# Attention scores of a graph layer with and without the target's linear term

## What is computed

```
h = _layer_norm(x, ln1_g, ln1_b)
xl = (h @ Wl).reshape(-1, HEADS, C)          # left: the source's rows
xr = (h @ Wr).reshape(-1, HEADS, C)          # right: the target's rows
e = einsum('ehc,hc->eh', leaky_relu(xl[src] + xr[dst], 0.2), att)
m = segment_max(e, dst);  ex = exp(e - m[dst])
alpha = ex / (segment_sum(ex, dst)[dst] + 1e-16)
out = segment_sum(alpha[..., None] * xl[src], dst) + gat_bias
```

## Time and profile before

| | us |
|---|---|
| timed, median of 3 | 1217.9 |
| timed, lowest and highest | 1214.75, 1218.52 |
| span of the profiled execution | 1275.0 |
| VectorE busy in the profiled execution | 1030.6 |
| TensorE busy in the profiled execution | 1089.3 |

### The profile page before, as it was taken

How to read it: one execution, slowest core, us unless ns; L and a number is a source line. 1 busy time by engine, 2 the same in 40 slices (tenths; PEclk the granted TensorE clock), 3 DMA queues, 4 the chain that set the end, 5 groups by cost and what they waited for, 6 DMA issues and landing times.

```text
span 1275.0 us, 16061 instructions
## 1 busy us (share of the span) xinstructions
PE 1089.3 (85%) x5027; PEld 793.4 (62%) x5047; DVE 1030.6 (81%) x1478; ACT 681.0 (53%) x1264; POOL 436.6 (34%) x412
## 2 busy tenths in 40 slices
PE   3979879566766666499999999799999999999998
PEld 2578456444544444245555555598888888889896
DVE  8999999778777887899999999876766869583934
ACT  4601300465565654478888888767555674232420
POOL 2072073565555666177766665000002100000000
PEclk9989989888777876599999999799999999999999
DMA  5000001566565658266667666400000211000002
GB/s 187 34 10 15 25 10 34 150 168 173 165 173 160 181 166 193 59 165 194 194 191 195 191 191 153 141 1 18 9 9 25 65 38 46 1 18 25 1 1 82
DMA packets 43436, 122.85 MB, mean 96 GB/s; under 512 B 7838, under 2 KB 8626, under 8 KB 43352
## 3 DMA queue, kind: packets, MB, share of 16 engines
q0 software_dynamic: 29184, 93.81, 27.5%
q1 hardware_dynamic: 14168, 27.98, 6.6%
HBM read 116.13 MB, written 5.59 MB: 95 GB/s over the span
## 4 chain that ended last, share of the span: by engine, by line
PE 46%; ACT 7%; DVE 2%; issue 1%; ACTq 1%; another core or an unknown queue 0%; DVEq 0%
PE bank L891 11%; PE bank L851 8%; PE bank L837 8%; PE bank L784 7%; PE bank L907 7%; PE bank L795 5%; ACT counts L1077 3%; ACT hot L964 2%; ACT arena L962 2%; PE bank L822 1%; ACTq L1073 0%; DVE stat L1269 0%; PE bank L625 0%; DVE w_lo L1637 0%
## 5 line engine op out<-in xcount | busy, mean ns | idle before, releaser
L587 POOL DMA_INDIRECT arena<-left_table,arena x352 | 356.8, 1013 | 235.7 <-issue 85.4
L784 PE MATMUL bank<-arena,hot 128*128 128x512 f32 x352 | 177.5, 620 | 0.9 <-DVE den_parts L1661 0.9
L718 PE MATMUL bank<-xr_hi,hot_t 128*128 x176 | 94.9, 539 | 97.3 <-ACT bank L1050 66.7
L1569 DVE SCALAR_TENSOR_TENSOR arena<-bank,arena 128x1024 f32<-128x1024 f32 x88 | 107.7, 1224 | 54.4 <-PE bank L718 29.9
L891 PE MATMUL bank<-counts_r,ns 128*128 128x512 f32 (+2 forms) x720 | 137.1, 349 | 0.0
L891 PEld LDWEIGHTS bank<-counts_r,ns 128*128 128x128 f32 x720 | 125.6, 188 | 10.4
L1077 ACT ACTIVATE counts<-bank 128x1280 f32 x88 | 108.9, 1238 | 37.6 <-issue 21.1
L795 PE MATMUL bank<-arena 128*128 128x512 bf16 (+1 forms) x508 | 110.0, 349 | 9.2 <-ACT counts L1077 5.6
L1050 ACT ACTIVATE bank<-arena 128x1024 f32<-128x1024 f32 x88 | 90.2, 1025 | 42.8 <-DMA arena<-left_table,arena 29.9
L718 PEld LDWEIGHTS bank<-xr_hi,hot_t 128*128 128x128 f32 x176 | 41.9, 238 | 110.4 <-issue 104.9
L1573 DVE TENSOR_REDUCE arena<-arena 128x16 f32<-128x1024 f32 x88 | 107.3, 1220 | 2.7
(11 more groups left out here) (258 smaller groups left out, 2256.2 us busy)
## 6 DMA issues: line engine op xcount, KB each, us to landing
arena<-left_table,arena POOLq DMA_INDIRECT x352
arena<-in_x_dram SPq DMA_DIRECT2D x18, 256.0 KB, 5.0
arena<-in_L_gnn_W_dram SPq DMA_DIRECT2D x8, 512.0 KB
arena<-in_L_gnn_W_dram SPq DMA_DIRECT2D x2, 1536.0 KB, 11.1
arena<-in_L_gnn_W_dram SPq DMA_DIRECT2D x3, 1024.0 KB, 5.3
left_table<-arena SPq DMA_DIRECT2D x10, 260.0 KB, 2.0
out_dram<-state SPq DMA_DIRECT2D x9, 256.0 KB
arena<-in_L_gnn_Wl_dram SPq DMA_DIRECT2D x1, 1024.0 KB, 9.0
```

The lines of the kernel that those rows point to most:

```text
L587: g.indirect_dma_start(out=gathered[n % DEPTH][:, i, :], out_offset=None, in_=left_table, in_offset=bass.IndirectOffsetOnAxis(ap=src_of[:, ...
L718: ins_ = t.matmul(bank[:, rows_at(n) + i, :], mine, part[:, bass.ds(at, 1), :].rearrange("p b n -> p (b n)"), start=False, stop=(part is x ...
L784: t.matmul(bank[:, psum, :], as_float(hot[c % 4]), w[:, i, :], start=(i == 0), stop=(i == 1))
L1569: v.scalar_tensor_tensor(y, bank[:, at:at + 2, :], 0.0, over(att_relu, 1, 2), ALU.max, ALU.mult).then_inc(*rows_weighted.up())
```

## The change

The target's linear term is no longer formed, added or stored; the softmax over the edges of a target is the same without it. With it go: the linear tile and the right half of wa; the product and the reduction on VectorE for the right side; half the columns of L658; two of ScalarE's three small copies per block, with the wait between them; the subtraction L1376; the two products L731 of each pair, linear_added, keep_targets and the waits for both; and the additions L1552 and L1558. tile_ready now counts one a block instead of two. lay_scores keeps one addition and runs at the pairs of LAY_AT (12, 23, 34, 45, 56, 67, 78 and 87), two tiles after the last of its 22 tiles. The arena's tiles behind linear and wa lie lower by their size.

```diff
@@ -90,10 +90,9 @@
 
     rows_at = lambda n: 2 * ((n + ZRING - 1) % ZRING)
     QUAD = 2 * PAIR
-    LINEAR_TILES = 256 // (2 * HEADS)
 
     RUNS = 2
-    ADD_AT = {min(NG - 1, LINEAR_TILES // 2 * -(-RUNS * SK * (u + 1) // LINEAR_TILES)): u for u in range(SG // RUNS)}
+    LAY_AT = {min(NG - 1, RUNS * SK * (u + 1) // 2 + 1): u for u in range(SG // RUNS)}
     COUNT_AT = 5 * 512
     W1_PARTS = 2 * KC
     BATCH, QUARTET = 16, 4
...
@@ -651,11 +648,11 @@
                         ins_.then_inc(*projected.up())
                         if side == 0:
                             yield
-                    t.wait_ge(att_folded.sem, 2)
+                    t.wait_ge(att_folded.sem, 1)
                     if b >= 2:
-                        t.wait_ge(tile_ready.sem, 2 * (b - 1))
+                        t.wait_ge(tile_ready.sem, b - 1)
                     for k in range(KC):
-                        ins_ = t.matmul(bank[:, 4 + b % 2, 0:2 * HEADS], trans[b % 3][:, k, :], wa[:, k, :, :].rearrange("p i h -> p (i h)"), start=(k == 0), stop=(k == KC - 1))
+                        ins_ = t.matmul(bank[:, 4 + b % 2, 0:HEADS], trans[b % 3][:, k, :], wa[:, k, :], start=(k == 0), stop=(k == KC - 1))
                     ins_.then_inc(*att_projected.up())
                     yield
 
...
@@ -718,21 +715,10 @@
                         ins_ = t.matmul(bank[:, rows_at(n) + i, :], mine, part[:, bass.ds(at, 1), :].rearrange("p b n -> p (b n)"),
                                         start=False, stop=(part is xr_lo), skip_group_check=True)
                 ins_.then_inc(*rows_added.up())
-                c = 2 * n
-                if c % LINEAR_TILES == 0 and c:
-                    t.wait_ge(targets_kept.sem, c // LINEAR_TILES)
-
                 for _ in range(2):
                     t.matmul(bank[:, 7, 256:512], iota_node[:, 0:P], iota_node[:, 0:256], start=True, stop=True)
-                for i in range(2):
-                    c = 2 * n + i
-                    mine = hot_t[n // 2 % 2][:, (n % 2 * 2 + i) * P:(n % 2 * 2 + i + 1) * P]
-                    at_column = c % LINEAR_TILES * 2 * HEADS
-                    ins_ = t.matmul(bank[:, 7, at_column:at_column + 2 * HEADS], mine,
-                                    linear[:, bass.ds(at, 1), :, :].rearrange("p b w h -> p (b w h)"), start=True, stop=True, skip_group_check=True)
-                ins_.then_inc(*linear_added.up())
-
-            t.wait_ge(tile_ready.sem, 2 * NB)
+
+            t.wait_ge(tile_ready.sem, NB)
             prime(range(KEY_BANKS, 2 * ZRING))
             spread_local(0)
             t.wait_ge(keys_laid.sem, 1)
...
@@ -987,12 +973,9 @@
                         if side == 0:
                             yield
                     a.wait_ge(*rows_kept.now())
-                    a.activation(xr_hi[:, b, :], as_float(xr_lo[:, b, :]), ACT.Copy)
+                    a.activation(xr_hi[:, b, :], as_float(xr_lo[:, b, :]), ACT.Copy).then_inc(*right_hi.up())
                     a.wait_ge(att_projected.sem, b + 1)
                     a.activation(tile[b % 2][:, D:TW], bank[:, 4 + b % 2, 0:HEADS], ACT.Copy).then_inc(*tile_ready.up())
-                    a.activation(as_float(linear[:, b, 1, :]), bank[:, 4 + b % 2, HEADS:2 * HEADS], ACT.Copy).then_inc(*tile_ready.up())
-                    a.wait_ge(*tile_ready.now())
-                    a.activation(linear[:, b, 0, :], as_float(linear[:, b, 1, :]), ACT.Copy).then_inc(*right_hi.up())
                     yield
 
             def x_root(nth, g):
...
@@ -1035,7 +1018,6 @@
                 a.activation(gap_t, bank[:, 6, :], ACT.Abs, bias=minus_own[:, :]).then_inc(*ao.up())
                 if m >= 2:
                     a.wait_ge(rows_added.sem, 2 * (m - 1))
-                    a.wait_ge(linear_added.sem, 2 * (m - 1))
                 a.wait_ge(*ao.now())
                 a.activation(hot_t[m % 2], gap_t, ACT.Relu, bias=ones[:, 0:1], scale=-1.0).then_inc(*hot_t_ready.up())
                 a.wait_ge(*hot_t_ready.now())
...
@@ -1050,18 +1032,11 @@
                 a.activation(bank[:, at:at + 2, :], gathered[n % DEPTH][:, :, 0:D], ACT.Copy).then_inc(*seeded.up())
                 a.activation(source_linear[:, 2 * n:2 * n + 2, :], gathered[n % DEPTH][:, :, D:TW], ACT.Copy).then_inc(*sources_kept.up())
 
-            def keep_targets(k):
-                c0, c1 = k * LINEAR_TILES, min(NC, (k + 1) * LINEAR_TILES)
-                a.wait_ge(linear_added.sem, c1 // 2)
-                a.activation(target_linear[:, c0:c1, :, :].rearrange("p c w h -> p (c w h)"), bank[:, 7, 0:(c1 - c0) * 2 * HEADS], ACT.Copy).then_inc(*targets_kept.up())
             target_hots(0)
             for n in range(NG):
                 seed(n)
-                if n % (LINEAR_TILES // 2) == 0 and n:
-                    keep_targets(n // (LINEAR_TILES // 2) - 1)
                 if n % 2 == 0 and n < NG - 2:
                     target_hots(n // 2 + 1)
-            keep_targets(targets_kept.value)
 
 
             def hot_of(c):
...
@@ -1372,8 +1347,7 @@
 
                 blocks = slice(first, end)
                 v.wait_ge(right_hi.sem, end)
-                v.tensor_tensor(xr_lo[:, blocks, :], as_float(xr_lo[:, blocks, :]), as_float(xr_hi[:, blocks, :]), ALU.subtract)
-                v.tensor_tensor(linear[:, blocks, 1, :], as_float(linear[:, blocks, 1, :]), as_float(linear[:, blocks, 0, :]), ALU.subtract).then_inc(*right_split.up(end - first))
+                v.tensor_tensor(xr_lo[:, blocks, :], as_float(xr_lo[:, blocks, :]), as_float(xr_hi[:, blocks, :]), ALU.subtract).then_inc(*right_split.up(end - first))
                 v.wait_ge(twice_normed.sem, end)
                 v.wait_ge(d_bias, 32)
                 v.tensor_tensor(state[:, blocks, :], state[:, blocks, :], over(gat_bias, 1, end - first), ALU.add).then_inc(*biased.up(end - first))
...
@@ -1397,14 +1371,13 @@
                 v.wait_ge(*vo.now())
                 v.scalar_tensor_tensor(x_shift[:, nth, blocks], x_moments[:, nth, blocks, 0], -1.0, x_scale[:, nth, blocks], ALU.mult, ALU.mult).then_inc(*x_scaled[nth].up())
 
-            def fold_weights(side, w):
-
-                v.wait_ge(d_w[side], 16)
+            def fold_weights():
+
+                v.wait_ge(d_w[0], 16)
                 v.wait_ge(*att_split.now())
-                p = products[side]
-                v.tensor_tensor(p.rearrange("p (k n) -> p k n", n=D), w, over(att_linear, 1, KC), ALU.mult).then_inc(*att_weighted.up())
+                v.tensor_tensor(products.rearrange("p (k n) -> p k n", n=D), w_left, over(att_linear, 1, KC), ALU.mult).then_inc(*att_weighted.up())
                 v.wait_ge(*att_weighted.now())
-                v.tensor_reduce(wa[:, :, side, :], p.rearrange("p (k h c) -> p k h c", k=KC, c=C), AX.X, ALU.add).then_inc(*att_folded.up())
+                v.tensor_reduce(wa, products.rearrange("p (k h c) -> p k h c", k=KC, c=C), AX.X, ALU.add).then_inc(*att_folded.up())
 
             def norm_x(first, end):
 
...
@@ -1461,8 +1434,7 @@
             v.tensor_scalar(att_relu, att_linear, 1.0 - SLOPE, None, ALU.mult).then_inc(*vo.up())
             v.wait_ge(*vo.now())
             v.tensor_scalar(att_linear, att_linear, SLOPE, None, ALU.mult).then_inc(*att_split.up())
-            fold_weights(0, w_left)
-            fold_weights(1, w_right)
+            fold_weights()
             norm_x(4, 5)
             count_digits(LOW)
             norm_x(5, NG2 + 3)
...
@@ -1544,19 +1516,10 @@
             def tiles_of(u):
                 return slice(RUNS * SK * u, RUNS * SK * (u + 1))
 
-            def add_linear(u):
+            def lay_scores(u):
 
                 c = tiles_of(u)
                 v.wait_ge(sources_kept.sem, c.stop // 2)
-                v.wait_ge(targets_kept.sem, -(-c.stop // LINEAR_TILES))
-                v.tensor_tensor(source_linear[:, c], source_linear[:, c], target_linear[:, c, 0, :], ALU.add).then_inc(*vo.up())
-
-            def lay_scores(u):
-
-                c = tiles_of(u)
-                v.wait_ge(*vo.now())
-                v.tensor_tensor(source_linear[:, c], source_linear[:, c], target_linear[:, c, 1, :], ALU.add).then_inc(*vo.up())
-                v.wait_ge(*vo.now())
                 ins_ = v.tensor_tensor(score_rows[:, :, RUNS * HEADS * u:RUNS * HEADS * (u + 1)].rearrange("p k (g h) -> p k g h", h=HEADS),
                                        score[:, c, :].rearrange("p (g k) h -> p k g h", k=SK), source_linear[:, c, :].rearrange("p (g k) h -> p k g h", k=SK), ALU.add)
                 if u == SG // RUNS - 1:
...
@@ -1567,13 +1530,11 @@
                 sc = score[:, 2 * n:2 * n + 2, :].rearrange("p i h -> p (i h)")
                 v.wait_ge(rows_added.sem, n + 1)
                 v.scalar_tensor_tensor(y, bank[:, at:at + 2, :], 0.0, over(att_relu, 1, 2), ALU.max, ALU.mult).then_inc(*rows_weighted.up())
-                if n in ADD_AT:
-                    add_linear(ADD_AT[n])
                 v.wait_ge(*rows_weighted.now())
```

(14 more changed lines are left out.)

## The result

The changed kernel takes 1213.35 us in the median of 20 runs (1210.46 to 1216.40), the kernel before, beside it, 1217.39 us (1213.80 to 1220.10, 20 runs): a ratio of 0.9966 with a 95% interval of 0.9957 to 0.9975. It is 4.1 us faster (3.0 to 5.2), inside the range of 1202 to 1217, in the direction that was forecast, and about two thirds of the 6.5 us of the sum. The 6.5 us of the sum and the 2.4 us of the rival in which the gathers are the floor both lie outside the interval, one on each side.

What follows compares the result with a forecast made beforehand. VectorE was taken to bound the opening and the score stage (2.50 us a pair, 88 pairs); 1.6 (fold) + 0.2 (L1376) + 4.7 (additions) = 6.5 us off 1217.9 gave 1211.4 us, range 1202 to 1217.

Steps and rivals of the forecast that it cites:

- the 6.5 us of the sum: Whole kernel: savings forecast on VectorE's path in the opening and score stage, 1.6 + 0.2 + 4.7 us; chance 0.50.
- the rival in which the gathers are the floor: Score stage: GpSimd's gathers also need 2.50 us a pair, so only 2.4 us is gained, 1215.5 us; chance 0.15.
- the holes: Score stage: idle stretches, 54.4 us on VectorE before L1569, held to be the profiled execution's; rival that they're real 0.13.
- The fold, 1.6 us: Opening: right weights' product and reduction leave VectorE, 4.52 us, of which 1.6 arrives; rival that all arrives 0.06.
- L1376, 0.2 us: Opening: the subtraction of the small halves, two instructions of at most 0.19 us, leaves the full VectorE, saving 0.2 us.
- ScalarE's copies and the halved product of the projection, 0: Opening: two of three copies per block go, hidden; TensorE's matmul has 8 columns instead of 16; no gain.
- L731 at 0: Score stage: two TensorE products per pair, 0.43 us at the low clock, go; hidden by VectorE's floor, gain 0.
- The additions, 8 x 0.59 = 4.7 us: Score stage: L1552 (0.14 us) and L1558 (0.45) leave VectorE, seven times in the loop and once at the end.
- The wait at the end, 0: Score stage's end: last addition's wait for L1056, taken as a hole; 0 in timed runs, 3.6 us as upper end.
- The rival of the clock: Score stage: fewer products lower TensorE's clock, 37 pairs lose 0.32 us each, 11.8 us in all, 1223.2 us; chance 0.11.

Runs made afterwards that it cites:

- additions_back: Changed kernel with two more VectorE operations of the old size at each of the eight LAY_AT pairs; 1215.15 us, ratio 0.9976 to the kernel before.
- spread_additions: Changed kernel with padding lanes gathering different rows and two more VectorE operations at each of eight pairs; 1212.93 us, ratio 0.9973 to the kernel before.
- no_constants: Changed kernel without each pair's two TensorE products on constants (L719), which nothing reads; 1215.70 us, ratio 0.9980 to the kernel before.

## Why the prediction was right, and where its sizes were off

The direction and the two parts that carry the gain were right. The range says less: it is 15 us wide and holds the 1215.5 us of the gathers' rival as well, so a time inside it does not single out the sum.

*What bounds the kernel.* Right: VectorE at about 2.5 us a pair, the holes a thing of one execution (4.2 us of idle time before the weighting in the second profile, 54.4 in the first). Missed: the last five pairs, where the gathers are the floor. Both profiles of before show it (in the first, the last packet of a gather of pair 87 ended 7.3 us after its issue, against 3.5 in the mean of those before pair 83), but I looked at calm stretches and at one hole, not at the end of the loop.

*The fold, 1.6 us.* Right in mechanism and nearly in size: 1.9 us at the first weighting (1.7 between the means of all profiles with and without the fold), 2.2 and 1.8 timed. ScalarE's L972 came 1.4 us earlier (44.59 to 43.15) where I had taken 0.90, and L991 behind it 2.2 (45.88 to 43.65), which is the 1.4 and the 0.69 it no longer waits. Of the 1.4 us, 1.16 is TensorE's idle time before it turns block 2 in the second profile of before (0.90 in the first), which is gone after, and 0.23 the earlier landing of the weights.

*L1376, 0.2 us, and ScalarE's copies and the halved product of the projection, 0.* Not tested alone. The first weighting's 1.9 us holds them all.

*L731 at 0.* Right within the runs: three pairs of kernels show no cost, 0.2 us in the mean with some 1.6 either way. keep_targets and TensorE's wait for it were not put back alone.

*The additions, 8 x 0.59 = 4.7 us.* Mis-sized twice. VectorE's own work shrank by 4.1 us, not 4.7: at the last pair of the second profile it is 457.80 - 454.72 = 3.08 us from weighting to last addition, after 454.38 - 451.81 = 2.57, so 0.51 a pair. In the loop a pair with additions took 3.27 us from weighting to weighting in five of seven cases of that profile and 2.77 us in all seven after, so 0.50. The 0.59 came from a pair of 3.35 us, in which L1560 followed L1558 by 0.45 us instead of 0.37. The larger part is that of those 4.1 us only about 1.2 reach the end (additions_back), because VectorE arrives earlier at gathers that are late for their own reason; with the gathers mended 4.0 do (spread_additions). The prediction had read the gathers' 2.50 us a pair from a calm stretch and taken it to hold to the end. So the rival in which the gathers are the floor was right for five pairs of 88, and those stand at the end, where nothing behind them can make use of a lead. What timing gives for the parts, 2.2 + 1.2 = 3.4 us, and the 4.1 of the whole agree within their intervals.

*The wait at the end, 0.* Right: 1.5 us of the wait of before's second profile is of the late gathers, not of L1056, and it grew.

*The rival of the clock.* Its mechanism exists, its price was wrong and the change didn't trigger it. The clock over the stage was 0.93 before and 0.92 after, and the means of the timed executions agree (0.950 and 0.952). With 0.74 in no_constants a 230 us stage has about half of its time at 1.2 GHz, some 46 pairs; at 0.32 us each that would be 15 us, and 1.7 were measured. The 0.32 us came from pairs behind a hole, where VectorE was already waiting. In a stretch of the changed kernel at the low level VectorE lost nothing, and its first wait of 0.2 us or more comes at 440 us:

```profile
282.00:291.50 9.50, 8.60 (x28) 5.65 (x29) 9.26 (x9) 5.49 (x11) 6.20 (x7) 0.50 0.69 194
```

The gathers run up to three pairs ahead, and in most pairs the products end before VectorE is ready, so they may take longer. The low level is not free, though: within most of these kernels the slower executions tend to be the ones with the lower mean clock (of the changed kernel 1216.40 us at 0.943 and 1210.73 at 0.960). Which of the two follows from the other is not shown. The Trainium skill (TensorE: Matmul & The Clock Gate, "A second HAM failure mode: psum-queue depth-cycling") ties swings of the clock to short idle times between groups of matmuls; by that rule, taken as the prediction took it, the change would have been slower. The traces agree that less work between the groups lowers the clock (no_constants), and don't agree that taking out L731 was enough for it.

## What to carry to other kernels

When an engine is at its floor over a loop, look at the loop's last few rounds before adding up what each round gains: a producer that is late only there can swallow much of what the other rounds gained. Padding is data too; let its lanes fetch different rows, and check in the DMA view whether time per packet rises where the padding begins. Of a single profile trust the durations, not its waits: two profiles of one kernel differed by 50 us in the idle time before one line.

## What the runs showed of the hardware

- A gather of 128 rows of 2080 bytes lands 3.7 us after its issue when the rows differ, 6.3 us in a row of gathers that all read one row; time per packet rises by half (0.18 to 0.27 us), that of the row packets alone from 0.23 to 0.41. Ten such gathers cost this kernel 3.2 us, ten more 5.2, each with some 2 us either way. Why one row read by all lanes is slow stays open.
- One profiled execution was about 60 us longer than the other profile of the same kernel (1275.0 and 1213.5 us), with releases of TensorE that came some 4 us after its records. No timed run showed anything like it. What held them back stays open.
- Two products of 256 columns a pair on data that nobody reads hold TensorE's clock at 0.92 instead of 0.74 over 230 us, and that was worth 1.7 us here, with 2.4 either way.
